# A two-layer cross-attention and expert network on one Trainium2 core: norm rows on ScalarE, a new order and phase end, and the mask as a spare row of keys and queries

## The reference, cut to what matters

```python
# x (64,128,256), ctx_768 (64,128,192), mask (64,128) bool; everything in float32
x = x + L0_xattn(layernorm(x), ctx_768, mask, Wq, Wk, Wv, Wo)      # 16 heads of 16, masked scores
x = x + L0_ffn(layernorm(x), w_switch, b_switch, w1, b1, w2, b2)   # 8 experts, top 1, capacity 512
x = x + L1_xattn(layernorm(x), ctx_768, ...)                       # 16 heads, own small FFN behind it
x = x + L1_ffn(layernorm(x), ...)                                  # six attention nodes, fused weights

# L0_xattn, the part that the change touches
q = (x @ Wq).reshape(B, N, 16, 16).transpose(0, 2, 1, 3)           # k, v alike from the context
scores = einsum('bhid,bhjd->bhij', q, k) * 16 ** -0.5
scores = where(mask[:, None, None, :], scores, -finfo.max)
out = einsum('bhij,bhjd->bhid', softmax(scores), v) ... @ Wo
```

## Time and profile before

| | |
|---|---|
| median of 3 runs | 4074.48 us (lowest 4071.28; one run, 10919.02 us, is an outlier) |
| the profiled execution | 4072.37 us, its span 4070.6 us |
| mean granted TensorE clock | 0.994 of full speed |
| PE, DVE, ACT, POOL busy over the span | 98%, 59%, 64%, 47% |
| first phase, PE busy between 200 and 600 us | 94 to 96% |
| first phase, POOL busy between 200 and 600 us | 86 to 91% |

### The profile page before, as it was taken

One profiled execution on the slowest core, in us unless ns is written; L12 is line 12 of the kernel. 1 busy time (PEld: TensorE's weight loads), 2 busy tenths in 40 slices (PEclk: granted clock), 3 DMA queues, 4 the chain that ended last, 5 costly groups with the idle time before them and its releaser, 6 DMA issues.

```text
span 4070.6 us, 100757 instructions
## 1 busy us (share of the span) xinstructions
PE 3991.0 (98%) x38276; PEld 3401.4 (84%) x38276; DVE 2391.8 (59%) x6184; ACT 2622.6 (64%) x11786; POOL 1928.9 (47%) x2011
## 2 busy tenths in 40 slices
PE   7999999999999999999999999999999999999998
PEld 6888876678888888888888888888888888888887
DVE  5777772026566666665656666665666665666654
ACT  6888881215666666666666666666666666666665
POOL 5888883103444444444444444444444444444434
PEclk9999999999999999999999999999999999999999
DMA  3232214521000000000000000000000000000000
GB/s 104 71 97 68 70 53 138 173 82 35 14 12 15 17 14 14 13 14 14 14 16 13 14 13 13 12 13 19 13 12 12 12 12 12 12 12 12 7 4 9
DMA packets 117866, 129.73 MB, mean 32 GB/s; under 512 B 12006, under 2 KB 110676, under 8 KB 117264
## 3 DMA queue, kind: packets, MB, share of 16 engines
q1 hardware_dynamic: 105648, 109.80, 8.5%
q0 software_dynamic: 6144, 8.43, 0.7%
q10 hardware_dynamic: 5600, 5.07, 0.4%
HBM read 89.68 MB, written 41.94 MB: 32 GB/s over the span
## 4 chain that ended last, share of the span: by engine, by line
PE 76%; DVE 1%; ACT 0%; POOL 0%; issue 0%; DMA 0%; POOLq 0%
PE c_product L1495 37%; PE c_product L1506 15%; PE c_product L1554 10%; PE c_scores L1544 7%; PE c_product L1577 5%; PE c_product L1565 2%; DVE c_qT L1350 1%; PE c_product L1483 1%; ACT c_front_probs L1307 0%; PE c_product L1614 0%; DMA out<-c_fin 0%; POOL c_fin L1291 0%; DVE c_nodes L1350 0%; POOL c_front_probs L1261 0%; ACT c_probsT L1313 0%
## 5 line engine op out<-in xcount | busy, mean ns | idle before, releaser
L1261 POOL TENSOR_TENSOR c_probs<-c_probs,c_row_inv 128x512 f32<-128x512 f32 x744 | 769.1, 1043 | 1358.2 <-DVE c_row_inv L1362 1353.0
L1307 ACT ACTIVATE c_probs<-c_scores,c_neg_max 128x128 f32<-128x128 f32 x2976 | 1050.2, 406 | 334.0 <-DVE c_neg_max L1359 334.0
L1495 PE MATMUL c_product<-c_nodes,cell_w 128*128 128x256 f32 x4352 | 1065.2, 383 | 2.8 <-DVE c_nodes L1421 2.3
L1495 PEld LDWEIGHTS c_product<-c_nodes,cell_w 128*128 128x128 f32 x4352 | 796.3, 190 | 121.4 <-DVE c_nodes L1350 8.3
L1359 DVE TENSOR_REDUCE c_neg_max<-c_scores 128x4 f32<-128x512 f32 x1024 | 658.2, 679 | 179.0 <-PE c_scores L1544 171.6
L1307 ACT ACTIVATION_READ_ACCUMULATOR c_probs<-c_scores,c_neg_max 128x1 f32 x2976 | 730.7, 246 | 0.0
L1313 ACT COPY c_probsT<-c_product 128x512 f32<-128x512 f32 x744 | 407.7, 601 | 435.8 <-PE c_product L1554 430.2
L1307 ACT ACTIVATE c_front_probs<-c_scores,c_neg_max 128x128 f32<-128x128 f32 x1120 | 398.7, 396 | 183.0 <-DVE c_neg_max L1359 183.0
L1261 POOL TENSOR_TENSOR c_front_probs<-c_front_probs,c_row_inv 128x512 f32<-128x512 f32 x280 | 294.5, 1055 | 292.0 <-DVE c_row_inv L1362 290.2
L1506 PE MATMUL c_product<-cell_w,c_nodes 128*128 128x256 f32 x1792 | 429.3, 379 | 0.0
L432 ACT ACTIVATE a_probs<-a_scores,a_neg_max 128x128 f32<-128x128 f32 x1024 | 361.2, 399 | 82.1 <-DVE a_neg_max L488 81.4
(11 more groups left out here) (177 smaller groups left out, 6505.7 us busy)
## 6 DMA issues: line engine op xcount, KB each, us to landing
e_w<-in_L_ffn_w SPq DMA_DIRECT2D x12, 1024.0 KB, 6.4
a_x<-in_x SPq DMA_DIRECT2D x32, 256.0 KB, 2.8
a_ctxT<-in_ctx_pairsT SPq DMA_DIRECT2D x32, 256.0 KB, 3.0
x<-a_x SPq DMA_DIRECT2D x32, 256.0 KB, 2.1
xn<-a_xn SPq DMA_DIRECT2D x32, 256.0 KB
c_routed<-xn SPq DMA_DIRECT2D x32, 256.0 KB, 2.7
c_x<-x SPq DMA_DIRECT2D x32, 256.0 KB, 3.1
c_ctxT<-in_ctx_pairsT SPq DMA_DIRECT2D x32, 256.0 KB, 2.8
```

Source lines behind the costliest of these rows:

```text
L1261: nc.gpsimd.tensor_tensor(e, e, rinv[:, i, r].unsqueeze(2).broadcast_to([P, 4, T]), ALU.mult).then_inc(norm_made, 1)
L1307: a = nc.scalar.activation(probs(n, j)[:, r, k], S[r][:, k], ACT.Exp, bias=nmax[:, i, r, k:k + 1], accum_out=rsum[:, i, r, k:k + 1])
L1495: i = T_.matmul(m[:, u], w[:, k, u * P:(u + 1) * P], src[:, k], start=n == 0, stop=n == last)
```

## The change

The steps, their arithmetic and the sizes of the projections stay. Four things change:

1. **The mask rides in the scores' own products.** The keys for the even heads have sixteen rows of zeros in each strip; one of them (row 16, for the odd heads row 0) now carries 0 or -2^127 per key token, and the queries carry 1 in the same row. The queries are therefore written twice (`qT_even`, `qT_odd`), by two instructions in place of one, and the keys by SCALAR_TENSOR_TENSOR instructions that add the mask rows. The four mask products of each round are gone, and with them the row of ones. The mask rows are made for two jobs at a time (two instructions of 128x512 for every second job) in place of four jobs at a time (one of 128x1024).
2. **`nm` goes to ScalarE**: two activations (Identity, scale and bias from SBUF). VectorE writes the negated mean behind `st`, and GpSimd multiplies it by the reciprocal deviation behind `rs` (both 128x2).
3. **New tables** for all four engines. The ring of second-norm rows grows from 6 to 8 jobs, `L`, `Tn` and `put` run up to two iterations later, and `K^` one iteration ahead of the other steps in its table.
4. **New ends** of the phase for TensorE and VectorE, and one for GpSimd.

```diff
 FIRST_PE_ORDER = """
-K:1 T0.1:3 S1:2 Tx:1 A:3 r.n:6 Q:1 O:3 T1.0:2 T0.0:2 S0:1 V:1 L:5 Tn:4 T1.1:2
+Tn:6 Q:1 T0.1:3 T1.1:3 S0:1 A:3 r.n:7 K:0 O:3 T1.0:2 T0.0:2 S1:1 L:6 Tx:0 V:1
 FIRST_POOL_ORDER = """
-rs:1 nm:1 rs1:4 S0.n0:2 nm1:4 S0.n1:2 S1.n0:2 S1.n1:2 S1.n3:2 S1.n2:2 S0.n3:2 S0.n2:2 put:9
+S0.n3:2 nm1:4 put:11 S0.n1:2 S1.n0:2 rs:0 S0.n2:2 S1.n1:2 S0.n0:2 S1.n2:2 S1.n3:2 rs1:3
+FIRST_POOL_TAIL = """
+put:8 rs1:1 nm1:1 put:7 put:6 put:5 put:4 put:3 put:2 put:1
...
-    X_RING, ROW_RING, GROUP = 4, 6, 4
-    MASK_JOBS, SENDS, RING = 4, 3, 3
+    X_RING, ROW_RING, GROUP = 4, 8, 4
+    MASK_JOBS, SENDS, RING = 2, 3, 3
...
+                    pool.wait_ge(rstd_made[0], j + 1)
+                    nc.gpsimd.tensor_tensor(shift[:, j % 2], neg_mean[:, j % 2], rstd[:, 0, j % 2], ALU.mult).then_inc(shift_made, 1)
...
+                elif n == "nm":
+                    act.wait_ge(shift_made, j + 1)
+                    if j >= 1:
+                        act.wait_ge(prod, n_prod["Tx", j - 1])
+                    for b in range(PAIR):
+                        k = nc.scalar.activation(xn[:, b], xt[:, j % X_RING, b], ACT.Identity, bias=shift[:, j % 2, b:b + 1],
+                                                 scale=rstd[:, 0, j % 2, b:b + 1])
...
-                    V.tensor_scalar(mkb[:, g % 2], mku[:, g % 2], 1.0, NEG, ALU.subtract, ALU.mult).then_inc(mask_made, 1)
+                    for h in range(2):
+                        spare = cst[:, C_SPARE + 3 * h:C_SPARE + 3 * h + 1]
+                        k = V.tensor_scalar(mkr[:, h], mku[:, g % 2], spare, spare, ALU.mult, ALU.subtract)
...
-                    V.tensor_scalar(qT[:, o], product(n, j), 0.25, None, ALU.mult).then_inc(prod_used, 1)
+                    for h, q in enumerate((qE, qO)):
+                        c = C_SPARE + 3 * h + 1
+                        k = V.tensor_scalar(q[:, o], m, cst[:, c:c + 1], cst[:, c + 1:c + 2], ALU.mult, ALU.add)
...
-                    V.tensor_scalar(kE[:, o], m, cst[:, C_EVEN:C_EVEN + 1], None, ALU.mult)
-                    V.tensor_scalar(kO[:, o], m, cst[:, C_ODD:C_ODD + 1], None, ALU.mult).then_inc(prod_used, 1)
+                    for h, (a, c) in enumerate(((kE, C_EVEN), (kO, C_ODD))):
+                        k = V.scalar_tensor_tensor(out=a[:, o], in0=m, scalar=cst[:, c:c + 1], op0=ALU.mult, op1=ALU.add,
+                                                   in1=mkr[:, h, t0:t0 + W2].unsqueeze(1).broadcast_to([P, 2, W2]))
...
-                        T_.matmul(S[r][:], one_row[g],
-                                  mkb[g, j // MASK_JOBS % 2, off:off + T].unsqueeze(1).broadcast_to([32, 4, T]),
-                                  start=True, stop=False)
...
+                            if k == 0 and (n, j) in round_before:
+                                n0, j0 = round_before[n, j]
+                                pe.wait_ge(exp_made, n_exp[f"{n0}.e{r}", j0])
-                            i = T_.matmul(S[r][:, k], qT[g, o, u, b * T:(b + 1) * T], w[g, o, u, b * T:(b + 1) * T],
-                                          start=False, stop=k == 3)
+                            i = T_.matmul(S[r][:, k], q[g, o, u, b * T:(b + 1) * T], w[g, o, u, b * T:(b + 1) * T],
+                                          start=True, stop=True)
```

More of the change, by code:

```diff
@@ L43, in consts_array @@
              np.full((P, 2), 1e-5), np.full((P, 2), 1e-6)]
+    for row in (16, 0):
+        spare = (i % 32 == row)[:, None]
+        parts += [spare * NEG, ~spare * 0.25, spare]
     return np.concatenate([np.asarray(a, np.float32) for a in parts], 1)
-C_ID, C_TRI, C_ONE, C_EVEN, C_ODD, C_IOTA, C_HALF, C_EPS5, C_EPS6, C_END = \
-    0, 128, 256, 384, 385, 386, 394, 396, 398, 400
+C_ID, C_TRI, C_ONE, C_EVEN, C_ODD, C_IOTA, C_HALF, C_EPS5, C_EPS6, C_SPARE, C_END = \
+    0, 128, 256, 384, 385, 386, 394, 396, 398, 400, 406
 BANKS = 4
@@ L183, in phase_first_layer @@
                                       (FIRST_PE_ORDER, FIRST_DVE_ORDER, FIRST_ACT_ORDER, FIRST_POOL_ORDER))
-    on_pe, on_dve = ended(FIRST_PE_TAIL, on_pe, JOBS), ended(FIRST_DVE_TAIL, on_dve, JOBS)
+    on_pe, on_dve, on_pool = (ended(tail, order, JOBS) for tail, order in (
+        (FIRST_PE_TAIL, on_pe), (FIRST_DVE_TAIL, on_dve), (FIRST_POOL_TAIL, on_pool)))
     def is_turn(n):
@@ L231, in phase_first_layer @@
         ct = sb("ctxT", [2, 2, W2])
-        mku, mkb = sb("mask_u8", [2, MASK_JOBS * W2], U8), sb("mask_add", [2, MASK_JOBS * W2], BF16)
-        one_row = sb("one_row", [P], BF16)
+        mku, mkr = sb("mask_u8", [2, MASK_JOBS * W2], U8), sb("mask_rows", [2, MASK_JOBS * W2], BF16)
         stats, mv = sb("stats", [2, PAIR, 6]), sb("mean_var", [2, 2, PAIR, 2])
         veps, rstd = sb("var_eps", [2, 2, PAIR]), sb("rstd", [2, 2, PAIR])
-        qT = sb("qT", [2, 2, W2])
+        neg_mean, shift = sb("neg_mean", [2, PAIR]), sb("shift", [2, PAIR])
+        qE, qO = sb("qT_even", [2, 2, W2]), sb("qT_odd", [2, 2, W2])
         kE, kO = first["kT_even"], sb("kT_odd", [2, 2, W2])
@@ L272, in phase_first_layer @@
         zero_made, buf_zeroed = sem("zero_made"), sem("buf_zeroed")
+        mean_made, shift_made = sem("mean_made"), sem("shift_made")
         step, shifted, exped, hot, slots_made = \
@@ L465, in statistics @@
                     k = V.bn_aggr(mv[:, i, j % 2, b], stats[:, i, b])
+                if i == 0:
+                    k.then_inc(mean_made, 1)
+                    dve.wait_ge(mean_made, j + 1)
+                    k = V.tensor_scalar(neg_mean[:, j % 2], mv[:, 0, j % 2, :, 0], -1.0, None, ALU.mult)
                 k.then_inc(var_made[i], 1)
@@ L470, in chain @@
                 dve.wait_ge(step, t_step.up())
-            for r in range(ROWS):
-                V.memset(one_row[32 * r:32 * r + 32], 0.0)
             dve.wait_ge(consts_in, 16)
             chain(V.memset(before[:, 0], 0.0))
-            for r in range(ROWS):
-                k = V.memset(one_row[32 * r:32 * r + 1], 1.0)
-            k.then_inc(ones_made, 1)
             chain(V.tensor_scalar(i8[:], cst[:, C_IOTA:C_IOTA + E], float(E), None, ALU.subtract))
@@ L637, in _ @@
                     b = int(n[1])
-                    pe.wait_ge(mask_made, j // MASK_JOBS + 1)
-                    for r in range(ROWS):
-                        if (n, j) in round_before:
-                            n0, j0 = round_before[n, j]
-                            pe.wait_ge(exp_made, n_exp[f"{n0}.e{r}", j0])
-                        g = slice(32 * r, 32 * r + 32)
-                        off = (PAIR * (j % MASK_JOBS) + b) * T
-                        T_.matmul(S[r][:], one_row[g],
-                                  mkb[g, j // MASK_JOBS % 2, off:off + T].unsqueeze(1).broadcast_to([32, 4, T]),
-                                  start=True, stop=False)
                     landed("Q", j)
```

33 lines of the change are left out of this document (19 added, 14 removed).

## The result

The changed kernel takes 4086.43 us (median of 8 runs, 4080.59 to 4091.91), the kernel before 4071.93 (also a median of 8): ratio 1.0035, interval 1.0025 to 1.0045. It is slower by 14 us, where 16 us of gain were forecast. Forecast: 4056, range 4030 to 4079.

A forecast was written before the change was run, and what follows sets the result against it. TensorE, 98% busy, was taken as the bound, with GpSimd a second bound close behind. From 4072.4 us, plain jobs gain 17, routing loses 4 and filling gains 3: 4056 us, range 4030 to 4079.

The forecast's parts named there:

- Mask products: TensorE's mask products in both rounds: 0.70 us a job, 0.12 of it kept, so 0.58 gained.
- The wait for the queries: TensorE's fourth transpose slot behind Q waits for VectorE's two query copies: 0.3 us a job lost.
- The mask rows: VectorE's two half-width instructions every second job: 0.5 us each, 0.5 a job, 0.3 more than before; its sum covered.
- The order and the norm: TensorE's wait for GpSimd's probabilities goes, 0.22 us a job gained; `st` waiting for x costs 0.1.
- GpSimd and ScalarE: Work per job: GpSimd falls from 16.70 to 14.5 us; ScalarE reaches 16.0 with two norm activations of 0.45 each.
- VectorE's other additions: VectorE's `K^` with mask operand stays at 0.750 us, adding 0; the negated mean adds 0.2.
- Routing: Routing groups cost 4.4 us above four plain jobs against 3.8, over 7 groups 4 us lost.
- Filling: While the phase fills, the first three jobs gain up to 1.5 us each, 3 us in all.
- End: The last job's chain up to the start of the experts: 0, at most 5 us either way.
- The first: VectorE, held up by GpSimd, becomes the bound from 3.4 us of holding a job: 4079 to 4105 us, chance 0.08.
- The second: Late x makes a new cycle, or ScalarE cannot be kept fed: jobs 17.6 to 17.8, 4066 to 4078 us, chance 0.22.
- The third: Everything fits: TensorE's list alone, 16.9 us a job, routing groups 2 to 3 us: 4034, at best 4025, chance 0.2.

The follow-up runs named there:

- experiment 9: Changed kernel with its spare row undone and the mask products then left out altogether, so scores are unmasked: 4052.76 us, 0.995 to the kernel before.
- experiment 10: Changed kernel with mask rows and the second copy of the queries made only for the first two jobs: 4047.12 us, 0.9945 to the kernel before.
- experiment 7: Changed kernel with only the spare row undone (mask products as before; new orders, phase end and norm on ScalarE kept): 4056.62 us, 0.9957 to the kernel before.
- experiment 2: Changed kernel with the mask-row pair moved in VectorE's list from ahead of the keys to behind the reciprocals of batch 0: 4068.11 us.
- experiment 1: Changed kernel with mask rows made only for the first two jobs and kept for all later ones: 4064.82 us, 0.9979 to the kernel before.
- experiments 4: Kernel before with only the first norm moved to ScalarE, ahead of the exponentials of round S1: 4224.0 us, 1.0374 to the kernel before.
- 8: Kernel before with only the first norm moved to ScalarE, ahead of the copy T1^3, five places earlier than first tried: 4073.09 us, 0.9998.
- Experiment 12: Changed kernel with the spare row undone and the norm back on GpSimd, so new order and phase end alone: 4074.49 us, 1.0006 to the kernel before.

## Why the prediction was wrong

**Mask products: mis-sized.** I counted 0.70 us a job and left 0.12 of it standing, a gain of 0.58. Of the rows I used, 0.47 and 0.23, the first belonged to the old order (why it was so long, no run shows); in the new order both are 0.22. And a product that is taken out does not give back its start-to-start time when the next one then shows its own start: 0.11 a round, 0.22 a job (experiment 9) instead of 0.58.

**The wait for the queries: seen, at half its size.** I worked out 0.3 us from two instructions of 0.75. They take 0.81 and 0.80: the second scalar operand is a pointer too. The row reports a wait of 0.40; the stage loses 0.60 (experiment 10: 0.59), since the transposes on both sides of the pause overlap less: the four from 294.03 take 0.56 us to the next product, where four in a row take 0.46 (1.84 for sixteen in 7). This single wait outweighs all that the removed products give.

**The mask rows: the step that failed.** "I take 0.5 each, 0.5 a job", and of VectorE: "Its sum is covered; its order is not, in two places". The sum was covered: VectorE has 14.26 us of work in a plain job of 17.20, and 15.57 with the pair in one of 18.20. The size of the pair and its place were wrong. I named two places where VectorE's order is not covered, and left out the one where the pair stands, directly ahead of the keys. VectorE's row there, in a plain job of the changed kernel:

```profile
282.41 0.75 DVE L532 SCALAR_TENSOR_TENSOR front_keys<-a_product,consts_sb,a_mask_rows 128x512 f32<-128x512 f32 x1 [0.54 <-PE a_product L651]
283.07 0.74 DVE L532 SCALAR_TENSOR_TENSOR a_kT_odd<-a_product,consts_sb,a_mask_rows 128x512 f32<-128x512 f32 x1
```

VectorE idles 0.54 us ahead of the keys and is done at 283.81; TensorE wants the bank after eight transposes, at 283.93 + 0.92 = 284.85. That is 1.6 us of room.

In a row without routing it is the size that fails. The pair takes 2.17 us in the row at 298.99, since GpSimd multiplies at that time, and 1.06 where it is not held (experiment 2); the 1.0 that I had put would have fitted into the 1.6, as an estimate from these rows. In the routing group it is the place. The pair takes 1.36 us there, hardly held, but the chain has used the room up: without the pair TensorE waits 1.38 us for the keys (experiment 1), with it 2.85. One pair of each group of four falls into the row with the position chain, over which I had not laid it. Cost of both: 21.6 us (experiment 1), most of the 30 us between the forecast 4056 and 4086. No run has the pair unheld at its old place, so the share of each is not measured.

**The order and the norm: mis-sized the other way.** Together they take 0.95 us off a plain job (17.79 to 16.84, experiment 7), where my terms had 0.22 for GpSimd's wait and, against it, 0.1 for x. Their own list was no measure: for the same products TensorE is busy 17.57 us in the old order and 16.84 in experiment 7, so 0.73 of what I read as work was the spacing of its products in that order; 0.25 of it is the one mask product (0.47 against 0.22), the rest I have not split. So the plain job came out at 17.20 as -0.95 - 0.22 + 0.59, and not as -0.58 - 0.22 + 0.3 + 0.1 - 0.2: a right number from wrong terms. Experiment 12 shows why the move of the norm is needed for it: with the norm GpSimd's work alone is longer than that job.

**GpSimd and ScalarE: right.** GpSimd has 14.36 us in a plain job (14.5 said), ScalarE 16.23 (16.0), the norm takes 1.09 to 1.22 us for its two activations (0.9). By the formula on the Trainium skill's page "ScalarE: Activation LUTs" they were an estimated 0.98. ScalarE did not become the bound. What I missed is that a list has no room by its sum alone: at the wrong place the same two activations cost 151 us more (experiments 4 and 8).

**VectorE's other additions: right.** `K^` with the mask operand takes 740 to 752 ns, the negated mean 170.

**Routing: right in kind, too small.** I said 4.4 us above four plain jobs. It is 6.1 with the pairs, 3.6 without (72.4 - 68.8), and ScalarE waits once for 3.47 to 3.56 us where I had about 3. The clock adds to it: the group's last interval is 20.51 us at 1.00, and 21.95, 23.72, 23.78 and 24.87 in the other four groups of six, 12 us in all. That is 2 us a group on average, and I had put 0.7. Without the pairs the clock stays at 1.00.

**Filling: wrong.** No gain: the first three intervals are 2.1 us shorter together, but the first output product comes 2.4 us later, and the fourth starts at 107.13 us, at 106.91 before. **End: right.** From the last output product to the experts 32.5 us against 31.4.

**The rivals.** The first had the mechanism: VectorE held by GpSimd in the mask rows. It had the wrong consequence, VectorE as the bound from 3.4 us of holding a job on; here 1.1 us of holding in a row with a pair (2.17 against 1.06) did harm, since the pair stands ahead of the keys. The measured 4086 lies in its range of 4079 to 4105, which I had given 0.08. The second had as its sign VectorE waiting for `a_x`: 7.4 us in 500, not the cause. The third's time (4034) needs what no version reached. No rival had an added instruction on the way to a bank.

## What to carry to other kernels

Price an added instruction by its place and by what runs beside it, not by its engine's sum: follow what stands behind it in its list to the engine that waits for that, and give it the gap that the row of that wait shows. A removed product is worth what the next one does not need again, here half of its start-to-start time. When one change bundles a gain (order and norm, -17 us) with a loss (spare row, +30), a stretch that agrees with the forecast proves nothing about the terms; undo one part at a time.

## What the runs showed of the hardware

- VectorE, 128x512 bf16 from uint8 by two pointer scalars: 514 to 542 ns between GpSimd's multiplications, up to 1261 among them. The Trainium skill, page "SBUF — State Buffer", has the port pair of the two engines as an exclusive lock; the trace agrees, and also in that `K^`, with its product in PSUM, was never held (740 to 752 ns in 28, in some half of them beside running multiplications). The negated mean of 128x2 took 169 to 190 ns in 28; where a multiplication was running at its start it ended within 0.2 us, so these rows do not show whether it can be held.
- VectorE, 128x512 from PSUM: 690 ns by a constant, 750 with one pointer scalar (a scalar read per partition from SBUF), 801 to 811 with two.
- TensorE: the first score behind transposes takes 0.33 us to the next where later ones take 0.22; a mask product of bf16 ahead of it takes that up and costs 0.22 itself.
- The granted clock fell to 0.50 behind waits of 1.11 or 1.12 and 2.85 us in four groups; behind waits of 1.11 and 2.85 at 336 to 342 us, and of 1.01 and 2.85 at 411 to 417, it stayed at 1.00, so these two waits alone do not decide it. Where the second was 1.38 us (experiment 1) it never fell.
